# A Mamba layer with a mixture of experts on one core: another order of all operations, with all sixteen rounds written out

## The chip, the cores and the metric

The kernel runs on one core of a Trainium2 chip. The core has five engines that run side by side, each with an instruction queue of its own: TensorE (matmuls, PE in the profile, with its weight loads as PEld), VectorE (DVE), ScalarE (ACT), GpSimd (POOL) and SyncE (SP), which here only issues transfers. They meet through semaphores: an instruction raises a counter, and another one waits until the counter has reached a value. The metric is the device time of one execution in microseconds (us), as the median of several runs; lower is better.

## The reference, cut to what matters

The input is 32 sequences of 256 tokens with 128 channels. Two sublayers follow each other, each with a layer norm ahead and a residual around it.

```python
xr = x @ W_in;  xi, res = split(xr, 2)              # 128 -> 2 x 256
u = silu(causal_conv(xi, 4 taps) + conv_b)
dbc = u @ W_x                                       # 8 of delta, 16 of B, 16 of C
delta = softplus(dbc[:8] @ W_dt + b_dt)
for n in range(16):                                 # states
    h_n[t] = exp(delta * A_n)[t] * h_n[t-1] + (delta * u * B_n)[t]
    y += h_n * C_n
x = x + ((y + u * D) * silu(res)) @ W_out

scores = norm(x) @ gate_w.T;  top 2 of 8, softmax over the two
x = x + sum over e in 0..7 of cw[:, e] * (silu(norm(x) @ w1[e].T) @ w2[e].T)
```

All eight experts are computed for every token and weighted with `cw`, which is zero for six of them.

## The kernel before, in words

The work is cut into 16 rounds, r0 to r15, of two sequences (512 tokens) each. One round goes through all of the computation, but the rounds are laid over each other as in a pipeline: in a steady stretch TensorE works on the convolution of round i, the rows and states of rounds i-1 and i-2, and the experts of rounds i-4 and i-3.

For each of the 16 states n of a round: TensorE spreads row n of B over the partitions (`row_b`, L1737, into one of two banks of `rows`), VectorE multiplies it by `du` (`inputs`, L1248) and runs the scan (`scan`, L1258), with the factors `dA` that ScalarE has made by two exps (`decay`, L872). GpSimd multiplies the state by its row of C (`outputs`, L551), and TensorE adds it up while turning it (`sum_states`, L1758, eight turns). `row_b(j, n)` waits for scan n-2. `skip_in` (L1747) begins the sum of a round with u * D, which `skip` on ScalarE makes.

For each of the 8 experts: two hidden units (`hidden`, L1806 on TensorE, two matmuls each, and L906 on ScalarE, silu into `hid`), then `expert` (L1829, 16 matmuls), then `weight_expert` on VectorE (L1340) and `add_expert` on GpSimd (L591). hidden(j, e, f) is unit f of expert e of round j.

Around them: `turn_x`, `convolve` (L1682), `project_gate` (L1692), `project_bcd` (L1701), `take_high`, `take_middle`, `delta_rank` (L1727), `turn_y`, `project_out` (L1779), `turn_x2` and `score` on TensorE; norms, copies, `gate_silu`, `soft_parts` on ScalarE; `gating`, `residual`, `top_two` and statistics on VectorE; `add_soft`, `times_u`, `routing` and the deviations on GpSimd.

Six PSUM banks are shared. Where TensorE writes a bank, it first waits for the last reader of what was in it; the `use_...` entries in its order name these readers, so `hidden(three, 1, 0, use_hid(three, 0, 0))` waits until silu has read hidden(., 0, 0).

ScalarE's functions lie in two tables: exp and ln in one, silu in the other. A load of a table (ACT_TABLE_LOAD) stands ahead of the first activation that needs another one. It is put there when the kernel is built, and for silu it carries the line of the activation behind it (L906). The waits of a hidden unit on ScalarE are these two:

```python
wait(act, expert_done, j.count(E, e - 1))
act.wait_ge(hid_projected, j.count(E * FH, FH * e + f + 1))
nc.scalar.activation(hid[:, e % 2, f, :], bank(place(HIDDEN, j, e, f)), ACT.Silu).then_inc(hid_ready, 1)
```

The order of each engine is written out by hand (or by a planner, of which the kernel shows only the outcome): the first rounds, then a body `round_(i)` that `run` repeats, then the end. `run` writes the first bodies out and puts pairs of the others into a loop of the engine; inside it a round's semaphore values come from registers, outside they are constants. On TensorE and ScalarE rounds 6 to 15 of the body are five passes of that loop.

Of the kernel before, what the change touches and what calls it, by code (L numbers as in the profile page):

```python
# [43 lines left out]
HIDDEN = ("hidden", ((0, 1), (0, 1), (1, 0), (0, 0), (1, 0), (0, 1), (0, 0), (1, 0)))  # L44
# [5 lines left out]
MOVED = {("expert", 1, 0): 5, ("expert", 1, 1): 3, ("expert", 1, 2): 2, ("expert", 1, 4): 3, ("expert", 1, 5): 2,  # L50
         ("expert", 1, 6): 3, ("expert", 1, 7): 4, ("expert", 2, 0): 1, ("expert", 2, 1): 0, ("expert", 2, 2): 3,
         ("expert", 2, 3): 5, ("expert", 2, 4): 3, ("expert", 2, 5): 2, ("expert", 2, 6): 4, ("expert", 3, 1): 0,
         ("expert", 3, 2): 0, ("expert", 3, 4): 0, ("expert", 3, 5): 0, ("expert", 3, 7): 0,
         ("hidden", 1, 0, 1): 3, ("hidden", 1, 1, 0): 4, ("hidden", 1, 1, 1): 0, ("hidden", 1, 2, 0): 2,
         ("hidden", 1, 2, 1): 1, ("hidden", 1, 3, 0): 4, ("hidden", 1, 4, 1): 4, ("hidden", 1, 5, 0): 5,
         ("hidden", 1, 6, 0): 4, ("hidden", 1, 7, 0): 5, ("hidden", 1, 7, 1): 1, ("hidden", 2, 0, 0): 1,
         ("hidden", 2, 1, 1): 2, ("hidden", 2, 2, 0): 3, ("hidden", 2, 2, 1): 4, ("hidden", 2, 3, 0): 5,
         ("hidden", 2, 3, 1): 2, ("hidden", 2, 4, 0): 4, ("hidden", 2, 4, 1): 2, ("hidden", 2, 5, 0): 1,
         ("hidden", 2, 5, 1): 4, ("hidden", 2, 6, 0): 5, ("hidden", 2, 7, 0): 3, ("hidden", 2, 7, 1): 5,
         ("hidden", 3, 2, 1): 1, ("hidden", 3, 3, 0): 1, ("hidden", 3, 3, 1): 1, ("hidden", 3, 4, 1): 1,  # L60
         ("hidden", 3, 5, 0): 1, ("project_out", 1): 0, ("project_out", 2): 0, ("score", 1): 2}
# [30 lines left out]
def mamba_moe(nc, x, W_in, conv_w, conv_b, W_x, W_dt, b_dt, A_log, D, W_out, gate_wT, w1T, w2T, out):  # L92
# [15 lines left out]
    def run(eng, body, first, stages, stop):  # L108

        loop_first = max(first, stages + 2)  # L110
        pairs = (min(rounds, stop) - loop_first) // 2
        for i in range(first, loop_first):
            body(Round(i))
        with eng.Fori(0, pairs) as it:
            body(Round(loop_first, it))
            body(Round(loop_first + 1, it))
        for i in range(loop_first + 2 * pairs, stop):
            body(Round(i))
# [2265 lines left out]
```

## Time and profile before

| | |
|---|---|
| median of 3 runs | 1091.44 us (1090.85 to 1091.58) |
| profiled execution | 1092.1 us, span 1090.0 us |
| mean granted clock of TensorE | 0.978 |
| busy, share of the span | TensorE 95%, weight loads 70%, VectorE 93%, GpSimd 88%, ScalarE 83% |
| transfers | 84.12 MB, 77 GB/s on average |

The span is the time from the first to the last instruction; the profiled execution's own time is 2.1 us more. A matmul's end in the profile is modelled, and matmuls overlap by some 0.16 us, so the start of one and the start of the next tell what it costs. A wait is shown in brackets with what released it.

### The profile page before, as it was taken

The numbers are of one execution on the slowest core, as the hardware profiler recorded it, in microseconds if no ns is written. First come the engines' busy times: TensorE is split into PE (matmuls) and PEld (weight loads), VectorE is DVE, ScalarE is ACT, GpSimd is POOL, SyncE is SP. The second block draws the span as 40 slices with busy tenths as digits, with TensorE's granted clock in tenths as the row PEclk, the third lists the DMA queues.
The fourth block names the chain that finished last, engine by engine and source line by source line (L and its number), as shares of the span: only waits on it lengthen the run. The fifth ranks groups of instructions, "written<-read, shape, count | busy, mean of one in ns | idle before, by whom it ended". The sixth has DMA issues, their size and how long they took to land.

```text
span 1090.0 us, 18707 instructions
## 1 busy us (share of the span) xinstructions
PE 1040.8 (95%) x6150; PEld 758.0 (70%) x6150; DVE 1017.5 (93%) x1057; ACT 907.1 (83%) x1379; POOL 959.6 (88%) x890
## 2 busy tenths in 40 slices
PE   7787789999999999999999999999999999989998
PEld 4445466677777777777776777777777776767776
DVE  5999999999999999999999999999999999999822
ACT  4987867988989999998989899899989989875533
POOL 4688886999999999999999999999999999799934
PEclk9698989999999999999999999999999999989999
DMA  5332111122040312204031311403130130320000
GB/s 202 137 127 77 71 48 79 59 108 78 1 158 28 127 59 103 82 9 173 3 126 58 126 58 40 145 0 126 58 136 39 66 109 0 137 87 11 11 8 14
DMA packets 37364, 84.12 MB, mean 77 GB/s; under 512 B 3320, under 2 KB 28208, under 8 KB 28976
## 3 DMA queue, kind: packets, MB, share of 16 engines
q1 hardware_dynamic: 36880, 83.06, 21.4%
q8 instruction: 25, 0.41, 0.2%
q14 instruction: 43, 0.35, 0.1%
q10 hardware_dynamic: 416, 0.30, 0.1%
HBM read 78.63 MB, written 4.72 MB: 76 GB/s over the span
## 4 chain that ended last, share of the span: by engine, by line
PE 83%; DVE 9%; issue 4%; ACT 3%; DMA 0%; POOL 0%; DVEq 0%; ACTq 0%; POOLq 0%
PE work L1829 19%; PE work L1806 18%; PE y_ps L1758 18%; PE work L1682 8%; DVE h L1258 6%; PE rows L1737 4%; PE work L1779 3%; PE work L1666 2%; PE work L1701 2%; PE rows L1829 2%; PE work L1692 2%; PE rows L1806 1%; DVE rows L1248 1%; PE y_ps L1747 1%; PE work L1727 1%
## 5 line engine op out<-in xcount | busy, mean ns | idle before, releaser
L551 POOL TENSOR_TENSOR h<-h,c_rows 128x1024 f32<-128x1024 f32 x256 | 599.9, 2364 | 53.5 <-DVE h L1258 53.2
L1258 DVE TENSOR_TENSOR_SCAN h<-dA,rows 128x1024 f32<-128x1024 f32 x256 | 579.0, 2276 | 1.1
L872 ACT ACTIVATE dA<-delta,a_neg 128x510 f32<-128x510 f32 x512 | 325.7, 707 | 7.9 <-DVE h L1258 4.4
L1248 DVE TENSOR_TENSOR rows<-du,rows 128x1024 f32<-128x1024 f32 x256 | 306.7, 1214 | 4.9 <-PE rows L1737 4.9
L1758 PEld LDWEIGHTS y_ps<-ident,h 128*128 128x128 f32 x2048 | 241.2, 144 | 62.3 <-issue 34.5
L1758 PE MATMUL y_ps<-ident,h 128*128 128x128 f32 x2048 | 270.0, 278 | 10.3 <-POOL h L551 10.3
L1829 PEld LDWEIGHTS work<-w,hid 128*128 128x128 f32 x1856 | 223.3, 193 | 34.5 <-ACT hid L906 18.9
L1806 PE MATMUL work<-x2T,w 128*128 128x512 f32 x474 | 240.2, 602 | 2.9 <-ACT u L790 2.3
L1829 PE MATMUL work<-w,hid 128*128 128x128 f32 x1856 | 229.1, 277 | 2.4 <-ACT hid L906 2.2
L906 ACT ACTIVATE hid<-work 128x512 f32<-128x512 f32 x237 | 139.3, 596 | 65.5 <-PE work L1806 63.7
L591 POOL TENSOR_TENSOR x<-x,weighted 128x512 f32<-128x512 f32 x127 | 161.9, 1274 | 19.6 <-DVE weighted L1340 19.2
L1806 PEld LDWEIGHTS work<-x2T,w 128*128 128x128 f32 x474 | 82.2, 191 | 56.8 <-issue 19.0
L1737 PE MATMUL rows<-parts,select 96*128 96x512 bf16 x256 | 100.2, 392 | 21.9 <-DVE h L1258 20.4
L1682 PE MATMUL work<-xnT,w_conv 128*128 128x512 f32 x256 | 116.1, 596 | 0.5 <-ACT xnT L782 0.3
L756 ACT ACT_TABLE_LOAD x74 | 94.9, 1283 | 1.3
L906 ACT ACT_TABLE_LOAD x56 | 71.8, 1283 | 22.5 <-PE work L1806 16.7
L1340 DVE TENSOR_TENSOR weighted<-work,cw 128x512 f32<-128x512 f32 x116 | 78.4, 676 | 9.1 <-PE work L1829 7.2
L1682 PEld LDWEIGHTS work<-xnT,w_conv 128*128 128x128 f32 x256 | 47.3, 190 | 49.0 <-issue 47.8
L1737 PEld LDWEIGHTS rows<-parts,select 96*128 96x128 bf16 x256 | 25.4, 99 | 56.3 <-DVE h L1258 28.4
L542 POOL TENSOR_TENSOR du<-delta,u 128x1024 f32<-128x1024 f32 x15 | 35.4, 2360 | 1.8 <-POOL delta L535 1.3
L535 POOL TENSOR_TENSOR delta<-du,soft 128x1024 f32<-128x1024 f32 x15 | 35.4, 2362 | 0.0
L790 ACT ACTIVATE u<-work,conv_bias 128x512 f32<-128x512 f32 x32 | 22.0, 687 | 15.5 <-PE work L1682 15.3
(147 smaller groups left out, 941.7 us busy)
## 6 DMA issues: line engine op xcount, KB each, us to landing
c_rows<-c_dram SPq DMA_DIRECT2D x64, 1024.0 KB, 5.0
x_in<-in_x SPq DMA_DIRECT2D x16, 256.0 KB, 3.0
x_again<-in_x SPq DMA_DIRECT2D x16, 256.0 KB, 3.4
out<-x SPq DMA_DIRECT2D x15, 256.0 KB, 2.6
w<-in_w1T SPq DMA_DIRECT2D x1, 1024.0 KB, 4.8
w<-in_w2T SPq DMA_DIRECT2D x1, 1024.0 KB, 7.0
h<-in_conv_w SPq DMA_DIRECT2D x1, 512.0 KB, 4.9
c_dram<-bcd SPq DMA_DIRECT2D x16, 32.0 KB, 1.6
```

The lines of the kernel that those rows point to most:

```text
L551: nc.gpsimd.tensor_tensor(at, at, c_rows[:, n, :].unsqueeze(1).broadcast_to([P, H, T]), ALU.mult).then_inc(c_used, 1)
L591: nc.gpsimd.tensor_tensor(x1[:, j.odd], x1[:, j.odd], weighted[:, e % 2], ALU.add).then_inc(expert_added, 1)
L756: nc.scalar.preload_act_table_set("natural_log_exp_and_others")
L872: last = nc.scalar.activation(two_seqs(dA[:, n % RING, half, :])[:, :, 1:], two_seqs(delta[:, half, :])[:, :, 1:], ACT.Exp, scale=a_neg[:, ...
L906: nc.scalar.activation(hid[:, e % 2, f, :], bank(place(HIDDEN, j, e, f)), ACT.Silu).then_inc(hid_ready, 1)
L1248: nc.vector.tensor_tensor(rows[:, n % 2], du[:, j.odd], rows[:, n % 2, H - 1, :].unsqueeze(1).broadcast_to([P, H, T]), ALU.mult).then_inc( ...
L1258: nc.vector.tensor_tensor_scan(h[:, n % RING].rearrange("p h t -> p (h t)"), dA[:, n % RING].rearrange("p h t -> p (h t)"), rows[:, n % 2] ...
L1682: last = nc.tensor.matmul(two_seqs(work[:, CONV[half], :]), w_conv[:, k, half * P:(half + 1) * P], xnT[:, :, k:k + SEQ], start=(k == 0), s ...
L1737: nc.tensor.matmul(rows[:, n % 2, H - 1, :], select[:, n, :], parts[:, j.odd, :], start=True, stop=True).then_inc(b_ready, 1)
L1758: last = nc.tensor.matmul(y_ps[:, half, b, :], h[:, n % RING, half, b * P:(b + 1) * P], ident[:, :], is_transpose=True, start=False, stop= ...
L1806: nc.tensor.matmul(bank(place(HIDDEN, j, e, f)), w1[:, e, f, :], x2T[:, j.odd, :], start=True, stop=True).then_inc(hid_projected, 1)
L1829: last = nc.tensor.matmul(token_bank(place(EXPERT, j, e))[:, b, :], hid[:, e % 2, f, b * P:(b + 1) * P], w2[:, f, e, :], start=(f == 0), s ...
```

## The change

The loop of `run` goes: every body is written out, with its semaphore values as constants. And the order on every engine is another one: in the first rounds, in the body and at the end. The cut between first rounds and body also lies elsewhere (TensorE's body now begins at `sum_states(two, 6)`), which by itself moves nothing. The bank tables HIDDEN and MOVED follow the order. No operation is added or taken away. The core of the diff, by engine:

```diff
-    def run(eng, body, first, stages, stop):
-        loop_first = max(first, stages + 2)
-        pairs = (min(rounds, stop) - loop_first) // 2
-        for i in range(first, loop_first):
-            body(Round(i))
-        with eng.Fori(0, pairs) as it:
-            body(Round(loop_first, it))
-            body(Round(loop_first + 1, it))
-        for i in range(loop_first + 2 * pairs, stop):
+    def run(body, first, stop):
+        for i in range(first, stop):
             body(Round(i))
```

TensorE, body (waits on the left of a name left out; the steps that only changed their list of readers too):

```diff
                 expert(four, 3, use_hid(four, 4, 1))
+                expert(four, 4, use_dt(one, 1), use_hid(four, 4, 0))
+                hidden(four, 5, 0, use_expert(four, 3))
+                row_b(two, 12)
                 sum_states(two, 8)
-                expert(four, 4, use_dt(one, 1), use_hid(four, 4, 0))
-                row_b(two, 12)
-                hidden(four, 5, 0, use_expert(four, 3))
                 sum_states(two, 9)
                 hidden(four, 5, 1, use_expert(four, 4))
                 row_b(two, 13)
...
+                hidden(four, 7, 0, use_hid(four, 6, 1))
+                hidden(four, 7, 1, use_x2T(three), use_expert(four, 5))
...
                 sum_states(two, 11)
-                hidden(four, 7, 0, use_x2T(three), use_expert(four, 5))
-                hidden(four, 7, 1, use_xnT(i), use_hid(four, 6, 1))
+                score(three, use_hid(four, 7, 1), use_x2T(three))
                 row_b(two, 15)
-                score(three, use_hid(four, 7, 0), use_x2T(three))
                 sum_states(two, 12)
+                expert(four, 6, use_xnT(i), use_hid(four, 7, 0))
                 row_b(one, 0)
-                expert(four, 6, use_hid(four, 7, 1))
...
-                sum_states(two, 13)
-                row_b(one, 1)
-                convolve(i, 1, use_expert(four, 6), use_hid(four, 7, 1), use_xnT(i))
-                row_b(one, 2)
-                expert(four, 7, use_u(i, 0), use_scores(three), use_hid(four, 7, 0))
+                row_b(one, 1)
+                convolve(i, 1, use_expert(four, 6), use_xnT(i))
+                expert(four, 7, use_u(i, 0), use_scores(three), use_hid(four, 7, 1))
+                row_b(one, 2)
+                sum_states(two, 13)
                 sum_states(two, 14)
+                row_b(one, 3)
...
-                row_b(one, 3)
                 hidden(three, 0, 1, use_expert(four, 7), use_u(i, 0), use_scores(three))
                 sum_states(two, 15)
-                row_b(one, 4)
                 hidden(three, 1, 0, use_hid(three, 0, 0))
                 hidden(three, 1, 1, use_hid(three, 0, 1))
                 skip_in(one)
+                row_b(one, 4)
...
                 sum_states(one, 0)
                 sum_states(one, 1)
-                sum_states(one, 2)
                 row_b(one, 5)
                 expert(three, 0, use_gated(two), use_hid(three, 1, 0))
                 hidden(three, 2, 0, use_gated(two), use_hid(three, 1, 1))
                 row_b(one, 6)
                 hidden(three, 2, 1, use_expert(three, 0))
+                sum_states(one, 2)
                 expert(three, 1, use_hid(three, 2, 0))
-                row_b(one, 7)
...
+                row_b(one, 7)
                 expert(three, 2, use_expert(three, 1))
+                take_high(i)
+                row_b(one, 8)
                 sum_states(one, 3)
-                take_high(i)
                 sum_states(one, 4)
-                row_b(one, 8)
                 take_middle(i)
+                project_out(two, ...)
+                hidden(three, 3, 0, use_low(i), use_hid(three, 2, 1))
+                row_b(one, 9)
+                sum_states(one, 5)
+                project_gate(i, 0, ...)
+                delta_rank(i, 0, use_hid(three, 3, 0), use_low(i))
```

In the order of before, the last six of these are project_out, row_b(9), hidden(3, 0), sum_states(5), project_gate(0) and delta_rank(0). VectorE's body now begins with inputs 0 and 1, then scans 0 and 1, and goes on more often by twos; gating stands ahead of scan 4 as before, residual ahead of scan 8, top_two behind scan 14. GpSimd's body takes add_soft ahead of outputs(12) instead of behind it, times_u behind add_expert(4), routing ahead of outputs(0) of the next round instead of behind its outputs(2). ScalarE's body takes post_norm ahead of hidden(6, 0), pre_norm behind it, copy_xnT behind hidden(7, 1) and skip between the two conv_silu. SyncE:

```diff
-                three, four, five, seven = (i.later(-k) for k in (3, 4, 5, 7))
-                load_again(five)
-                load_c(four, 2)
-                store_c(three)
-                store_out(seven)
-                load_c(four, 3)
-                load_c(three, 0)
-                load_c(three, 1)
+                one, two, five = (i.later(-k) for k in (1, 2, 5))
+                load_c(two, 0)
                 load_x(i)
+                load_c(two, 1)
+                load_c(two, 2)
+                load_again(two)
+                store_c(one)
+                store_out(five)
+                load_c(two, 3)
```

Of the first rounds (TensorE, then ScalarE) and of the end (VectorE, then TensorE), what the prediction speaks of:

```diff
             row_b(r[0], 3)
+            row_b(r[0], 4)
+            skip_in(r[0])
+            row_b(r[0], 5)
             sum_states(r[0], 0)
...
-            skip(r[0])
             decay(r[0], 0)
...
             decay(r[0], 10)
+            skip(r[0])
...
-            weight_expert(r[14], 0)
...
             inputs(r[15], 15)
+            weight_expert(r[14], 0)
             scan(r[15], 15)
...
             expert(r[12], 6, use_hid(r[12], 7, 0))
             row_b(r[15], 0)
+            row_b(r[15], 1)
+            expert(r[12], 7, use_scores(r[13]))
+            row_b(r[15], 2)
             sum_states(r[14], 13)
...
+            hidden(r[14], 2, 1, use_expert(r[14], 0))
             sum_states(r[15], 15)
-            hidden(r[14], 2, 1, use_scan(r[15], 15))
```

## Rows read from the trace of the kernel before

**Rows 1.** The page: the chain that ended last, shares of the span by engine.

```profile
PE 83%; DVE 9%; issue 4%; ACT 3%; DMA 0%; POOL 0%; DVEq 0%; ACTq 0%; POOLq 0%
```

**Rows 2.** Busy time by stretch (columns in its first row).

```profile
core 0: us, PE busy (x) PEld busy (x) DVE busy (x) ACT busy (x) POOL busy (x), PEclk, DMA share, GB/s
31.60:60.00 28.40, 21.68 (x82) 12.76 (x83) 28.37 (x21) 25.73 (x41) 23.52 (x28) 0.76 0.21 65
...
204.89:269.55 64.66, 63.16 (x383) 46.20 (x383) 62.89 (x65) 57.48 (x89) 59.98 (x55) 1.00 0.22 79
332.50:395.25 62.75, 62.75 (x384) 46.45 (x383) 62.29 (x65) 57.53 (x88) 59.75 (x55) 1.00 0.24 81
395.25:458.48 63.23, 63.16 (x384) 46.18 (x383) 62.66 (x65) 57.72 (x89) 60.12 (x55) 1.00 0.22 80
...
1030.00:1090.00 60.00, 56.88 (x347) 42.51 (x346) 15.00 (x39) 22.76 (x39) 26.84 (x35) 1.00 0.04 10
```

**Rows 3.** Timeline of TensorE, looped round: start, duration, what, idle before.

```profile
606.23 1.02 PE L1806 MATMUL work<-x2T,w 128*128 128x512 f32 x2
...
608.44 2.05 PE L1829 MATMUL work<-w,hid 128*128 128x128 f32 x16
```

**Rows 4.** Timeline of TensorE, written round, the same place.

```profile
226.81 1.02 PE L1806 MATMUL work<-x2T,w 128*128 128x512 f32 x2
...
229.95 2.02 PE L1829 MATMUL work<-w,hid 128*128 128x128 f32 x16 [1.04 <-ACT hid L906]
```

**Rows 5.** Timeline of ScalarE, looped round, the same place.

```profile
606.49 1.28 ACT L906 ACT_TABLE_LOAD   x1 [0.74 <-PE work L1829]
607.79 1.31 ACT L906 ACTIVATE hid<-work 128x512 f32<-128x512 f32 x2
```

**Rows 6.** Timeline of ScalarE, written round, the same place.

```profile
227.92 1.28 ACT L906 ACT_TABLE_LOAD   x1 [1.53 <-PE work L1806]
229.21 1.08 ACT L906 ACTIVATE hid<-work 128x512 f32<-128x512 f32 x2
```

**Rows 7.** Timeline of TensorE, written round: hidden(1; 3, 0) and delta_rank(4; 0).

```profile
239.94 1.02 PE L1806 MATMUL work<-x2T,w 128*128 128x512 f32 x2
...
243.08 0.59 PE L1727 MATMUL work<-parts,w_dt 96*128 96x512 bf16 x2 [0.38 <-ACT hid L906]
```

**Rows 8.** Timeline of TensorE, written round, from hidden(1; 0, 0) to hidden(1; 1, 0).

```profile
215.57 1.02 PE L1806 MATMUL work<-x2T,w 128*128 128x512 f32 x2
216.43 0.38 PE L1737 MATMUL rows<-parts,select 96*128 96x512 bf16 x1
216.65 1.02 PE L1806 MATMUL work<-x2T,w 128*128 128x512 f32 x2
217.51 1.03 PE L1758 MATMUL y_ps<-ident,h 128*128 128x128 f32 x8
218.38 0.38 PE L1737 MATMUL rows<-parts,select 96*128 96x512 bf16 x1
218.62 1.55 PE L1806 MATMUL work<-x2T,w 128*128 128x512 f32 x3
```

**Rows 9.** Timeline of TensorE, written round: hidden(1; 5, 0) and hidden(1; 6, 0).

```profile
254.23 1.02 PE L1806 MATMUL work<-x2T,w 128*128 128x512 f32 x2
...
257.28 1.12 PE L1806 MATMUL work<-x2T,w 128*128 128x512 f32 x2
```

**Rows 10.** VectorE's waits from 31.6 to 204.9: us, times, longest.

```profile
DVE rows L1248 <- PE rows L1737: 2.9, 4, 1.4
```

**Rows 11.** Timeline of TensorE, end of the middle.

```profile
965.92 1.09 PE L1758 MATMUL y_ps<-ident,h 128*128 128x128 f32 x8 [2.63 <-POOL h L551]
...
969.02 0.61 PE L1737 MATMUL rows<-parts,select 96*128 96x512 bf16 x1 [1.65 <-DVE h L1258]
```

**Rows 12.** Timeline of VectorE, end.

```profile
978.60 1.23 DVE L1248 TENSOR_TENSOR rows<-du,rows 128x1024 f32<-128x1024 f32 x1 [1.17 <-PE rows L1737]
...
1029.59 0.67 DVE L1340 TENSOR_TENSOR weighted<-work,cw 128x512 f32<-128x512 f32 x1
```

More of the change, by code:

```diff
@@ L445, in _ @@
             load_c(r[3], 0)
+            load_again(r[3])
             load_c(r[3], 1)
-            load_x(r[6])
-            run(sp, round_, 7, 7, 19)
-            load_again(r[14])
+            load_c(r[3], 2)
+            store_c(r[4])
+            store_out(r[0])
+            load_c(r[3], 3)
+            run(round_, 6, 17)
+            load_c(r[15], 0)
+            load_c(r[15], 1)
             load_c(r[15], 2)
@@ L935, in round_ @@
                 hidden(four, 5, 1)
+                post_norm(three)
+                hidden(four, 6, 0)
                 pre_norm(i)
-                hidden(four, 6, 0)
-                post_norm(three)
                 hidden(four, 6, 1)
                 copy_x2T(three)
-                copy_xnT(i)
-                skip(one)
                 hidden(four, 7, 0)
                 hidden(four, 7, 1)
+                copy_xnT(i)
                 decay(one, 0)
@@ L951, in round_ @@
                 conv_silu(i, 0)
+                skip(one)
                 conv_silu(i, 1)
@@ L960, in round_ @@
                 decay(one, 7)
+                decay(one, 8)
+                decay(one, 9)
+                hidden(three, 2, 0)
+                hidden(three, 2, 1)
+                decay(one, 10)
+                decay(one, 11)
+                high(i)
+                copy_bcd(i)
+                decay(one, 12)
+                middle(i)
+                decay(one, 13)
             def lead_in():
@@ L1345, in round_ @@
                 three, four, five, six = (i.later(-k) for k in (3, 4, 5, 6))
-                inputs(four, 14)
-                scan(four, 13)
-                scan(four, 14)
-                top_two(five)
-                inputs(four, 15)
                 inputs(three, 0)
-                scan(four, 15)
-                weight_expert(six, 6)
+                inputs(three, 1)
                 scan(three, 0)
-                inputs(three, 1)
                 scan(three, 1)
@@ L1390, in round_ @@
                 weight_expert(five, 5)
+                inputs(three, 14)
+                scan(three, 13)
+                scan(three, 14)
+                top_two(four)
+                inputs(three, 15)
+                scan(three, 15)
+                weight_expert(five, 6)
             def split_dt_weights():
@@ L2135, in _ @@
[L2135 to L2141 removed]
+            expert(r[0], 4, use_gate(r[3], 0))
+            hidden(r[0], 5, 0, use_expert(r[0], 3))
+            sum_states(r[2], 8)
+            hidden(r[0], 5, 1, use_expert(r[0], 4))
+            delta_rank(r[3], 0, use_hid(r[0], 5, 0))
```

759 lines of the change are left out of this document (382 added, 377 removed).

## Prediction

> **What bounds the kernel now.** I read four views in this order. The chain of work that ended last says that TensorE carries 83% of the span and VectorE 9% [rows 1]. An average over stages can mislead, so I then cut the span into stretches, one from each round's first convolution to the next one's [rows 2]. There the reader is to see three things. In the steady part TensorE is busy for 62.75 of 62.75 us and VectorE for 62.29: both are full, TensorE sets the pace and VectorE has under half a microsecond to spare. Rounds alternate between 62.75 and 63.23 us, and the longer one holds the jump back of TensorE's loop, so the jump costs 0.43 to 0.48 us for every two rounds. The round from 204.89 us, where ScalarE's instructions are written out and the order on all engines is that of the loop, takes 64.66 us. That is 1.9 us more for the same work, and it is the row on which this prediction turns: why is the written round slower?
>
> The timeline of TensorE answers where. In the looped round expert(., 1) starts 2.21 us after hidden(., 2, 0) started [rows 3]; in the written round 3.14 us [rows 4], with 1.04 us named as a wait for ScalarE's `hid`. The timeline of ScalarE answers why. In the loop the activation table is loaded at 606.49, while hidden(., 2, 0) (begun at 606.23) is still running; the load was released by the expert's matmuls, that is by `expert_done`, and silu starts at 607.79, 1.56 us behind its matmul [rows 3, 5]. In the written round the load starts at 227.92, released by the hidden matmul itself (L1806), and silu starts at 229.21, 2.40 us behind its matmul [rows 4, 6]. So with waits on constants the table load stands behind the wait for `hid_projected`; with waits on registers it stands ahead of it. The code of `hidden` is the same. The 1.28 us of the load come into the path from TensorE to ScalarE and back each time silu's table is loaded for a hidden unit that has just been computed.
>
> The other places in a written round: delta_rank(., 0) starts 3.14 us after hidden(., 3, 0) [rows 7]; hidden(., 1, 0) starts 3.05 us after hidden(., 0, 0) [rows 8]; hidden(., 6, 0) starts 3.05 us after hidden(., 5, 0) [rows 9]. These distances, 3.05 to 3.14, are the same loop each time: 2.40 to silu, 0.60 for silu, the rest for the signal. Each stop, however short, also makes the matmuls behind it start some 0.1 us later: hidden(., 2, 1) to expert in the loop has such a row (2.05 us for an expert's 16 matmuls where an undisturbed one takes 1.95).
>
> **The change part by part.** TensorE's own work is not changed. From [rows 8] a hidden unit takes 0.86 us from start to start, a row of B 0.22, the 8 turns of one state 0.87; a gate projection takes the same 0.86 as a hidden unit. A steady round without its stop of 0.37 (0.27 before the expert, 0.10 after it, from [rows 3] against 0.86 + 0.22 + 0.86 = 1.94) is 62.75 - 0.37 = 62.38 us.
>
> *All rounds written out, and the new order of the middle.* Now every round has the late table load. What each place costs follows from what the new order puts between the two ends:
> - hidden(0,0) to hidden(1,0): two rows of B are taken out of this stretch (row 3 goes ahead, row 4 behind skip_in). Left are 0.86 + 0.86 + 0.87 = 2.59 us against the 3.05 needed: 0.46, and 0.10 behind it, 0.56.
> - hidden(2,0) to expert(1): sum_states(2) comes in, 1.94 + 0.87 = 2.81 against 3.05 to 3.14: 0.24 to 0.33, and 0.10, about 0.38.
> - hidden(3,0) to delta_rank(0): row 9 comes in, 0.86 + 0.22 + 0.87 + 0.86 = 2.81 against 3.14: 0.33.
> - hidden(5,0) to hidden(6,0): sum_states(8) and row 12 come in, 3.9 against 3.05: nothing.
> - turn_x2 to hidden(7,1) are now 1.30 us apart (four turns, half of a state's, and a hidden unit), about what a copy between them needs: bounded by nothing and the 0.1 of a short stop; I take nothing.
>
> The sum is 1.27, with the last bound 1.3 us a round. A check of the method on the written round of before: 1.20 + 0.10 at the expert, 3.14 - 2.59 = 0.55 at delta_rank, 0.24 + 0.10 at hidden(6,0), 0.10 behind hidden(1,0) give 2.29, and 64.66 - 62.38 = 2.28. So a new steady round is 62.38 + 1.3 = 63.7 us on TensorE. VectorE (62.3) and GpSimd (59.8) stay below that [rows 2].
>
> Twelve rounds of the expert work (those of r1 to r12) follow this pattern: 12 x 1.3 = 15.6 us. They lose what they had before: ten looped ones 0.37 each, 3.7; two written ones (r1, and r12 at 920 us, whose rows repeat those of r1) 2.28 and 2.2, 4.5; and the four jumps back of the five iterations, 4 x 0.43 = 1.7. Together 9.9, so the middle becomes 15.6 - 9.9 = 5.7 us longer.
>
> *Moves inside VectorE, GpSimd and SyncE.* VectorE's order now makes two inputs and then two scans more often. Its sum is the same, and a row of B is made at least 0.2 us before each input asks for it when I lay the starts of the new TensorE order beside the old ones; where it is not, VectorE now has 63.7 - 62.3 = 1.4 us a round to absorb it. The largest single delay of a row is that of row 4 (2.6 us), and its input also moves behind two scans. If that cover were gone it would cost VectorE those tenths. GpSimd moves routing ahead of outputs(0) and add_soft ahead of outputs(12); it has 3 us a round free. On SyncE, load_c(., 3) stands behind store_c and store_out, but is issued near scan 7 and read at scan 12; load_x now stands behind load_c(., 0). With the DMA engines busy for 0.22 to 0.24 of a round [rows 2] I cost these at nothing.
>
> *The first rounds.* The operations up to the steady part are the same, in an order that starts r0's experts earlier. In this stretch VectorE is full, so what can be won is its idle time: up to 204.9 us it waits 2.9 us for rows of B [rows 10]. The new order puts row 13 of r1 ahead of the convolution of r3 and hidden(0,1) ahead of sum_states(10), which speaks for fewer of these waits. Against it: skip(r0) on ScalarE stands behind eleven decays instead of ahead of them, and row 5 of r0 behind skip_in, in a stretch where the clock granted is 0.76 (matmuls at the lower of its two levels) [rows 2], where a turn of a state takes twice as long. Not shown by the trace; bounds are -2.9 (all these waits gone) and +2 (two more of a microsecond, as the longest here, 1.4). I take -1.0, nearer to the second bound than to the first since the clock works against it.
>
> *The end.* At 965.92 TensorE waits 2.63 us for a state from GpSimd and at 969.02 1.65 us for a scan, its clock drops, and VectorE then waits 1.17 us at 978.60 for row 4 of r15 behind hidden units [rows 11, 12]. In the new order expert(12,7) goes ahead of sum_states(14,13), expert(13,0) ahead of row 4, and input 4 stands behind weight_expert(13,0), so I take VectorE's 1.17 as gone. It gains weight_expert(14,0) ahead of the last scan, 0.6 [rows 12]. Behind the last sum_states TensorE has one hidden unit less, 0.86. So -1.17 + 0.6 - 0.86 = -1.4. Bounds: -3 (TensorE also keeps its clock) and +1 (the waits stay and only the weighting is added).
>
> **Sum.** 5.7 - 1.0 - 1.4 = +3.3 us on the profiled execution, 1092.1 us (span 1090.0), so 1095.4. The median of the runs is 0.66 lower: 1091.44 + 3.3 = 1094.7 us.
>
> The trace puts a table load at 1.28 us and silu 0.01 us behind it [rows 5, 6]. The Trainium skill (ScalarE: Activation LUTs, What ACT_TABLE_LOAD costs) gives 1283 ns for the load and about 1380 ns more for a drain at each switch. By the page, three late loads a round would cost another 3 x 1.38 us in each of twelve rounds; the trace agrees on the load and has no such drain, so the sum goes by the rows.
>
> **The rivals.**
> - *The new order has no stops from the late load* (this ends faster). Mechanism: the load is placed ahead of the wait again, or ScalarE is ready earlier than I read. For it: in the loop silu is 1.56 us behind. Against it: every written hidden unit with a load shows 2.40. Then the middle is 12 x 0.15 - 9.9 = -8.1 and the time 1091.44 - 8.1 - 2.4 = 1081. It decides from the stop per round: at (9.9 + 2.4) / 12 = 1.0 us the change is worth nothing, below 0.85 it is faster.
> - *Unrolling pays*: the jumps go, which the alternation of 62.75 and 63.23 us speaks for [rows 2], and the stops are half of what I count, which no row speaks for: 12 x 0.65 - 9.9 - 2.4 = -4.5, 1087. The Trainium skill (Runtime: NRT & Kernel Launch, Instruction fetch mechanics) says that a taken branch breaks sequential prefetch and that kernels prefer full unrolling. The trace agrees that the jump costs something, 0.43 us each.
> - *The gains at the ends cover the stops*: first rounds -2.9, end -3, 5.7 in the middle: -0.2, 1091.2, no difference. For it: the waits are there. Against it: all of it would have to go.
> - *The first rounds get worse*: +2, and the end gives nothing: 5.7 + 2 = +7.7, 1099.
> - *The written stream is too long to be fetched in time*: against it, the written last 60 us have TensorE busy for 56.88 [rows 2], with only known waits. I give it 2 in 100.
>
> **Chances.** Forecast (a longer middle, partly paid back) 0.45; worse first rounds or more stops 0.13; gains at the ends cover it 0.24; half the stops 0.10; no stops 0.08. A measurement of this kernel tells about 0.2%, 2.2 us, from no change. Faster 0.18, within it 0.26, slower 0.56. The likeliest case alone spans 1093 to 1098 (1.1 to 1.45 us a round). The range reaches into the others: 1086 to 1100.
>
> **What would show it.** Right: tables before silu in all rounds starting about 1.1 us behind the hidden matmul, silu 2.40 behind; waits for `hid` in each round before hidden(1,0), expert(1) and delta_rank(0); all steady rounds alike, 63.5 to 63.9 us, no alternation; VectorE idle 1.4 us a round. Wrong: steady rounds under 63.4; a table load released by `expert_done`; or a first stretch that reaches the convolution of r4 more than 3 us away from 204.7.

## The result and the profile after

The changed kernel takes 1103.11 us (1101.34 to 1103.72) beside 1091.51 us (1090.85 to 1092.08) for the kernel before in the same session: ratio 1.0107 [1.0092, 1.0122]. The direction is as predicted, and the time lies 3.1 us above the range. The profiled execution has a span of 1101.9 us and its own time is 1103.68 us, so it is to be set against 1090.0 and 1092.1.

The chain that ended last, by engine (it answers [rows 1]). ScalarE's share has grown from 3% to 12%: TensorE's way now leads through it.

```profile
PE 77%; ACT 12%; issue 5%; DVE 4%; POOL 2%; ACTq 0%; DVEq 0%; POOLq 0%
```

Busy time by stretch, columns as in [rows 2], cut from one round's first convolution to the next one's. The rounds at 335.8 and 399.6 answer to those at 332.5 and 395.25. They are alike, 63.80 us each, and TensorE is busy for 63.18 of it. (Busy time runs to a matmul's end, so it also covers part of a short stop.)

```profile
31.60:60.00 28.40, 17.20 (x82) 12.20 (x83) 26.01 (x23) 23.09 (x39) 20.32 (x24) 0.68 0.22 68
...
207.60:271.70 64.10, 63.48 (x383) 45.84 (x382) 63.59 (x66) 57.92 (x89) 59.84 (x55) 1.00 0.22 79
335.80:399.60 63.80, 63.18 (x383) 45.97 (x382) 62.79 (x65) 57.56 (x88) 59.58 (x55) 1.00 0.22 79
399.60:463.40 63.80, 63.18 (x383) 45.98 (x382) 62.79 (x65) 57.56 (x88) 59.86 (x55) 1.00 0.22 80
```

TensorE's timeline at hidden(2, 0), sum_states(2) and the expert of a steady round (it answers [rows 3, 4]). From 485.06 to 488.20 are 3.14 us, though the work in between is only 2.81.

```profile
485.06 1.02 PE L1835 MATMUL work<-x2T,w 128*128 128x512 f32 x2
485.92 0.38 PE L1766 MATMUL rows<-parts,select 96*128 96x512 bf16 x1
486.14 1.02 PE L1835 MATMUL work<-x2T,w 128*128 128x512 f32 x2
487.00 1.04 PE L1787 MATMUL y_ps<-ident,h 128*128 128x128 f32 x8
488.20 0.46 PE L1858 MATMUL work<-w,hid 128*128 128x128 f32 x2 [0.16 <-ACT hid L935]
```

ScalarE at the same place (it answers [rows 5, 6]): the load begins 1.10 us and silu 2.40 us behind the start of the matmul, the two distances of the written round of before.

```profile
486.16 1.28 ACT L935 ACT_TABLE_LOAD   x1 [0.87 <-PE work L1835]
487.46 1.09 ACT L935 ACTIVATE hid<-work 128x512 f32<-128x512 f32 x2
```

TensorE between hidden(0, 0) and hidden(1, 0) (it answers [rows 8]): hidden(0, 0) and (0, 1), the turns of a state, and then the wait; 474.47 to 477.52 are 3.05 us where the work is 2.59.

```profile
474.47 1.88 PE L1835 MATMUL work<-x2T,w 128*128 128x512 f32 x4
476.19 1.04 PE L1787 MATMUL y_ps<-ident,h 128*128 128x128 f32 x8
477.52 1.55 PE L1835 MATMUL work<-x2T,w 128*128 128x512 f32 x3 [0.29 <-ACT hid L935]
```

**Where the 11.9 us arose.** The starts of some convolutions on TensorE's timelines, and the ends of the spans, of both kernels and of the experiments told below, in us:

```
                     conv r1  conv r4  conv r15    end   r4 to r15  r15 to end
before                  48.5    204.7     898.9  1090.0     694.2     191.1
changed                 54.9    207.6     910.0  1101.9     702.4     191.9
e1  before, written     47.9    204.7     916.2  1107.4     711.5     191.2
e2  changed, looped     54.0    206.5     917.7  1108.3     711.2     190.6
e3  changed, early      53.6    204.7     893.6  1083.3     688.9     189.7
e4  before, wr., early  48.4    204.3     893.6  1083.2     689.3     189.6
e5  as e2, loop at 6    54.2    206.3     922.8  1112.0     716.5     189.2
e6  first rounds        48.9    205.9     911.6  1103.2     705.7     191.6
e7  first, early        48.5    204.4     897.7  1087.5     693.3     189.8
e8  before, early       48.8    204.7     895.5  1084.1     690.8     188.6
e9  skip first          52.3    204.7     907.1  1099.0     702.4     191.9
e10 weight late         53.2    205.2     907.7  1100.0     702.5     192.3
e11 early, skip, weight 52.2    203.2     892.1  1082.3     688.9     190.2
e12 before, loop at 7   47.6    204.4     898.4  1089.4     694.0     191.0
e13 changed, PE written 53.9    206.4     899.0  1088.3     692.6     189.3
e14 before, ACT written 48.0    205.0     916.0  1107.3     711.0     191.3
```

The last two columns are differences of the rounded starts and can be off by 0.1.

Against the kernel before, the changed one loses 2.9 us up to the convolution of r4, 8.3 from there to the one of r15, and 0.7 from there to the end (from the unrounded starts). In the same cut the forecast was -1.0, +6.6 (eleven of the twelve rounds) and -2.3 (the twelfth with the end).

### The profile page after: what moved, and what is told of

It is laid out like the page before. It is cut to its first block, busy times and chain, and to the rows that moved or that the text cites. A ratio compares the mean times of both kernels' runs of the same rounds, so it can differ in the third digit from the quotient of the medians.

```text
span 1101.9 us, 17455 instructions
## 1 busy us (share of the span) xinstructions
PE 1043.0 (95%) x6150; PEld 752.3 (68%) x6150; DVE 1021.4 (93%) x1057; ACT 906.6 (82%) x1379; POOL 958.3 (87%) x890
## 4 chain that ended last, share of the span: by engine, by line
PE 77%; ACT 12%; issue 5%; DVE 4%; POOL 2%; ACTq 0%; DVEq 0%; POOLq 0%
PE work L1858 18%; PE work L1835 16%; PE y_ps L1787 15%; PE work L1711 8%; PE rows L1766 4%; ACT dA L901 4%; ACT L935 2%; ACT hid L935 2%; DVE h L1287 2%; PE work L1695 2%; PE work L1808 2%; PE work L1730 2%; PE rows L1858 2%; PE rows L1835 1%; PE work L1721 1%
## 5 line engine op out<-in xcount | busy, mean ns | idle before, releaser
L1787 PE MATMUL y_ps<-ident,h 128*128 128x128 f32 x2048 | 262.2, 276 | 6.3 <-POOL h L550 6.3
L1835 PE MATMUL work<-x2T,w 128*128 128x512 f32 x474 | 237.7, 601 | 5.8 <-ACT hid L935 3.8
L1721 PE MATMUL work<-xnT,w_in 128*128 128x512 f32 x64 | 34.7, 625 | 1.6 <-issue 0.8
```

Of the source, the lines that this page charges most:

```text
L1787: last = nc.tensor.matmul(y_ps[:, half, b, :], h[:, n % RING, half, b * P:(b + 1) * P], ident[:, :], is_transpose=True, start=False, stop= ...
L1835: nc.tensor.matmul(bank(place(HIDDEN, j, e, f)), w1[:, e, f, :], x2T[:, j.odd, :], start=True, stop=True).then_inc(hid_projected, 1)
```

## The experiments

**e1: the order of before, its loops written out.** The functions `run` are replaced by those of the changed kernel, nothing else.

```diff
-            run(act, round_, 5, 4, 16)
+            run(round_, 5, 16)
...
```

> The order of the kernel before, its loops written out with constants; nothing else is changed. Theory (the silu table is loaded behind the wait for the matmul as soon as waits are constants): the ten looped rounds go from 62.97 us on average to the 64.66 us of the written round of before, +16.9, so about 1108 us, and every silu with a load starts 2.40 us behind its matmul. Rival (the form is free and only the order decides): the four jumps go, about 1.7 us less, 1089.8 us.

Measured: 1109.67 us (1107.84 to 1110.67), ratio 1.0155 [1.0136, 1.0173], steady rounds 64.65. Writing out costs the order of before 17 us; the new order, at 1103.11, is the better of the two for written rounds.

**e2: the changed order with the loops of before.**

```diff
-            run(round_, 5, 16)
+            run(pe, round_, 5, 5, 16)
...
```

> The new order with the loops of the kernel before (rounds 7 to 14 or so in loops). Theory: the looped rounds lose the late table load, 63.80 us each becomes about 62.7 with the jump shared out, some 8 to 10 rounds, so 1092 to 1095 us; what is left over the kernel before (1 to 4 us) is the new first rounds. Rival (the order itself causes the 63.8): the looped rounds stay at 63.8 plus the jump, 1105 us.

Measured: 1110.21 us (1109.28 to 1110.79), 1.016 [1.0143, 1.0177]. Both expectations missed. From convolution to convolution the looped rounds without TensorE's jump take 62.7 to 62.8 us, as the theory has it; those with one take 67.8 to 69.5. TensorE's timeline around the first jump:

```profile
496.58 0.60 PE L1763 MATMUL work<-parts,w_dt 96*128 96x512 bf16 x2
501.22 1.96 PE L1794 MATMUL y_ps<-ident,h 128*128 128x128 f32 x8 [4.05 <-issue]
```

"issue" says that TensorE waited for nothing that the profile shows. The trace's record of the taken branch there lasts 4.90 us, the two later ones 4.37 and 5.02; in the kernel before the four last 0.24, 0.22, 0.21 and 0.21. The eight turns behind the gap take 1.96 instead of 1.04 us.

**e3: the changed kernel with silu's table asked for ahead of both waits**, in `hidden`, `conv_silu` and `gate_silu`.

```diff
+            def silu_tables():
+                if tables[0] != "silu":
+                    nc.scalar.preload_act_table_set("silu_and_others")
+                tables[0] = "silu"
...
-                tables[0] = "silu"
+                silu_tables()
```

> The changed kernel with the silu table loaded explicitly ahead of both waits of the activation that needs it. Theory: the stops of 0.56, 0.41 and 0.32 us go in all rounds, a steady round is 62.4 to 62.6 us instead of 63.80, twelve rounds, so 15 us less, about 1088 us; first rounds stay some 5 us late. Rival (the load costs ScalarE the same wherever it stands, or silu is held by something else): 1103 us, silu still 2.40 us behind its matmul.

Measured: 1085.29 us (1084.91 to 1086.21), 0.9935 [0.9919, 0.9952]: 17.8 us less than the changed kernel by this one request in three places, and faster than before. ScalarE's timeline at the place of the rows above; the load now lies under the matmul (which begins at 476.59), and silu starts 1.53 us behind it:

```profile
476.82 1.28 ACT L791 ACT_TABLE_LOAD   x1
478.12 1.27 ACT L941 ACTIVATE hid<-work 128x512 f32<-128x512 f32 x2
```

Its TensorE, without a stop ahead of the expert at 479.41:

```profile
476.59 1.02 PE L1841 MATMUL work<-x2T,w 128*128 128x512 f32 x2
...
478.54 1.03 PE L1793 MATMUL y_ps<-ident,h 128*128 128x128 f32 x8
479.41 0.39 PE L1864 MATMUL work<-w,hid 128*128 128x128 f32 x2
```

Busy time of e3 in a window of the length of a steady round (62.57 us from convolution to convolution). TensorE is busy throughout and VectorE for 62.45 of 62.60: what is left in the middle is the work itself.

```profile
330.30:392.90 62.60, 62.60 (x383) 45.96 (x383) 62.45 (x65) 57.78 (x88) 59.96 (x55) 1.00 0.22 81
```

**e4: e1 with the same early table**, the edit of e3 on the written order of before.

> The order of before, written out, with the silu table loaded explicitly ahead of both waits. Theory: no stops from the load and no jumps: steady rounds of 62.4 to 62.8 us, and the two written rounds of before (64.66) fall to the same, so 1091.5 - 10 x 0.4 - 2 x 2 = 1083 to 1085 us. Rival (loading earlier only moves the time): as e1, about 1108 us.

Measured: 1084.75 us (1083.10 to 1085.64), 0.9925 [0.9908, 0.9942]. 25 us less than e1 for the same edit. With the table early the two orders are equal: rounds of 62.64 and 62.57 us.

**e5: e2 with TensorE's loop at another place.** By the code of `run` it begins at round 6 here and at round 7 in e2, so one round less is written out ahead of it; the expectation names the rounds wrongly, and the body that repeats is two rounds, not three.

```diff
-            run(pe, round_, 5, 5, 16)
+            run(pe, round_, 5, 4, 16)
```

> Changed order with its middle looped as in the second experiment, but TensorE's loop begins at round 6 instead of round 5 (one round more written out ahead of it, the same body of three rounds). If the 4.4 to 5.0 us of TensorE's taken jumps there come from where the loop's code lies, the jump changes: below 1 us each, and the time falls to about 1092 to 1098. If they come from the length of this loop's body or from its being a loop at all, they stay at 4 to 5 us each, and the time stays at 1108 to 1111.

Measured, in a single run: 1114.12 us. The four taken branches last 4.54, 4.29, 4.88 and 4.60 us. Whether the loop begins at 6 or 7 doesn't decide it.

**e6: the changed kernel with the first rounds of before** on TensorE, ScalarE, VectorE and GpSimd. For TensorE, the head of it:

```diff
             lead_in()
-            project_gate(r[0], 0, use_u(r[0], 0))
             row_b(r[0], 0)
+            project_gate(r[0], 0, use_u(r[0], 0))
             row_b(r[0], 1)
+            skip_in(r[0])
...
```

> Changed kernel with the order of the first rounds (up to the steady part) of the kernel before on TensorE, ScalarE, VectorE and GpSimd. Theory, that the new first rounds cost 5.1 us up to the scans of r3: the scan (r3, 0) begins at 208 to 209 instead of 213.4, steady rounds stay 63.8, and the time is 1097 to 1099 against 1103.1. Rival, that VectorE or TensorE make it up later in any case (no gain at the end): 1102 to 1104.

Measured: 1105.01 us (1102.97 to 1105.33), 1.0118 [1.0101, 1.0135]: no gain. The convolution of r1 starts at 48.9, 6.0 us earlier than in the changed kernel; at r4 1.7 us are left of that; and the round of r4 then takes 67.4 us instead of 64.1. The scan (r3, 0) begins at 211.7 us, where the theory had 208 to 209. TensorE there stops for 1.9 us ahead of row 4 of r3 and for 1.2 us ahead of expert(1, 1), where the changed kernel stops for nothing and 0.33 us. So the new middle doesn't fit behind the old first rounds, and this run doesn't price the first rounds by themselves.

**e7: e6 with the early table.**

> The sixth experiment's order with the silu table loaded ahead of both waits, as in the third. Theory, that the two add up: 1085.3 less 2.6 us (what the scan (r3, 0) of the third experiment, 210.4, is behind 208.2 of the fourth, with steady rounds of 62.57 against 62.64, -0.8 us in twelve rounds): 1082 to 1084, even with or up to 2 us below the fourth experiment's 1084.75. Rival, the two overlap or the joint adds waits: 1085 to 1087.

Measured: 1087.38 us (1087.03 to 1089.33), 0.9965 [0.9951, 0.9979]: 2 us more than e3 and 0.4 above the rival's band; the theory that the two add up has failed. The round of r4 takes 67.4 us, as in e6.

**e8: the kernel before with nothing but the early table**, loops kept.

> Kernel before, its loops kept, with nothing but the early load of the silu table. Theory: the ten looped rounds had the load ahead of the wait already, so they lose at most their stop of 0.37; the two written ones lose 2.28 and 2.2; the four jumps of 0.43 stay: 1092 less 4.5 to 8.2, so 1084 to 1088. Rival, the loop gains nothing and only the written rounds do: 1087 to 1088.

Measured: 1085.25 us (1083.91 to 1086.21), 0.9939 [0.9922, 0.9955]. From the convolution of r4 to that of r15 it takes 690.8 us, the kernel before 694.2: 1.9 us of the difference lie in the written round from r4 to r5 and 1.5 in the ten looped ones, 0.15 each, less than their stop of 0.37. The other 2.6 us of the profiled difference lie behind the convolution of r15, where the instructions are written out again.

**e9: the changed kernel with skip(r0) ahead of the decays.**

```diff
             lead_in()
+            skip(r[0])
             decay(r[0], 0)
...
-            skip(r[0])
```

> Changed kernel with one step moved back: skip(r0) stands ahead of the eleven decays on ScalarE again, as in the kernel before. Theory A, that this is what makes the first rounds late and that the lateness is carried through: skip_in(r0) no longer waits 4.1 us, the convolution of r1 starts at 49 to 51 us instead of 54.9, the one of r4 at 205 to 206 instead of 207.6, and the time is 1100 to 1101.5. Theory B, that the start of r0 is absorbed before the steady part and the late tables of the first rounds are what the 2.9 us at the convolution of r4 are: the convolution of r1 comes earlier all the same, the one of r4 stays within 1 us of 207, and the time is 1102 to 1103.7.

Measured: 1100.76 us (1100.04 to 1101.98), 1.0089 [1.0075, 1.0103]. Beside e10, whose first rounds are those of the changed kernel and which ran on the same chip, the convolution of r1 comes 0.9 us earlier and that of r4 0.5. But e10's first scan also begins 0.7 us earlier than e9's (30.1 and 30.8 us); counted from it, the two convolutions come 1.6 and 1.2 us earlier, and set against the mean of the five executions with the changed kernel's first rounds and late tables both come 2.1 us earlier. The time is 1.7 us below e10's and fell into theory A's band, and skip_in(r0) no longer waits. Of the places, r4's convolution (204.7) lies just below the band of 205 to 206, and r1's (52.3) is later than 49 to 51. Theory A holds in the main: skip is worth 1 to 2 us.

**e10: the changed kernel with the weighting behind the last scan.**

```diff
-            weight_expert(r[14], 0)
             scan(r[15], 15)
+            weight_expert(r[14], 0)
```

> Changed kernel with weight_expert(14,0) behind the last scan again. Theory: VectorE sets the pace in the last scans, so the last scan ends 0.6 us earlier and the end follows: span 1101.3, time 0.4 to 0.8 us less than 1103.1. Rival: TensorE has the expert's work to do in any case, and the hidden units that fill the gap make it no matter: last scan 0.6 earlier, end within 0.2 us of 1101.9.

Measured: 1102.45 us (1101.79 to 1103.18), 1.0105 [1.0090, 1.0121]. Counted from the convolution of r15, the last scan starts at 129.0 us instead of 129.6 and the span ends at 192.3 instead of 191.8. The time, 0.7 us less than the changed kernel's, lies in the theory's band, but not by its mechanism: in the profiled execution what the scan wins isn't handed on, and the end comes 0.5 us later; what is shorter there lies ahead of the convolution of r4.

**e11: e3 with both moves**, skip first and the weighting behind the last scan.

> The third experiment (changed order, silu's table loaded ahead of both waits) with the two steps of the ninth and tenth moved back. Theory A of the ninth: 1 to 2 us less than the third experiment's 1085.3, and 0.6 for the weighting: 1082.8 to 1084.2. Theory B: only the weighting, 1084.5 to 1085.3. Either would be about the time of the order of before with the same early tables, 1084.75.

Measured: 1085.21 us (1084.11 to 1085.82), 0.9945 [0.9932, 0.9959]. That is in theory B's band and not distinguishable from e3, e4 and e8. The convolution of r4 starts at 203.2 us, the earliest of all, 1.5 us ahead of e3; but the profiled execution is the fastest of its five (1084.11 to 1085.82), and the medians of e3 and e11 are equal. The end takes 190.2 instead of e3's 189.7, as in e10 longer with the weighting behind the scan.

**e12: the kernel before with TensorE's loop at round 7.**

```diff
-            run(pe, round_, 5, 4, 16)
+            run(pe, round_, 5, 5, 16)
```

> Kernel before with TensorE's loop beginning at round 7 instead of 6 (four passes instead of five, rounds 6 and 15 written out on TensorE). If the 0.2 us that its taken jump costs goes with what lies around the jump's target and not with the kernel, the jump changes to several microseconds and the time rises by 3 x 4 to 5 us to some 1104 to 1107. If it stays at 0.2 us: 1091 to 1093.

Measured, in a single run: 1091.21 us. The three taken branches last 0.24, 0.21 and 0.21 us. TensorE's timeline at the first: the matmul behind the jump comes 0.44 us after the one ahead of it, which lasts 0.38.

```profile
489.75 0.38 PE L1717 MATMUL work<-parts,minus 96*96 96x512 bf16 x1
490.19 1.04 PE L1779 MATMUL work<-w_out,yT 128*128 128x128 f32 x7
```

**e13: the changed order, looped on every engine but TensorE.** The edit is that of e2, but for TensorE.

```diff
-            run(round_, 5, 16)
+            run_written(round_, 5, 16)
...
```

`run_written` is the changed kernel's `run` under another name.

> Changed order with the loops of the second experiment on every engine but TensorE, whose rounds stay written out. The 4.4 to 5.0 us of TensorE's jumps cannot come up, and ScalarE waits on registers in its loop, with the table ahead. Theory (the late table on ScalarE is what the middle costs, and the order alone costs about what the first rounds do): all looped rounds at 62.8 to 62.9 us like the second experiment's undisturbed ones, no jump, the end as in the changed kernel; 1110.2 less 3 jumps of 5 to 6.5 us: 1091 to 1095. Rival (writing TensorE out costs time itself): 1098 to 1103.

Measured: 1090.34 us (1089.46 to 1091.14), 0.9985 [0.9975, 0.9994]. Slightly less than the theory's band. Busy time in two windows of a round's length (its looped rounds take 62.7 to 62.9 us from convolution to convolution):

```profile
397.00:459.80 62.80, 62.80 (x384) 45.96 (x384) 62.36 (x65) 57.89 (x89) 60.02 (x55) 1.00 0.23 81
459.80:522.60 62.80, 62.80 (x383) 45.95 (x382) 62.47 (x65) 57.73 (x88) 60.07 (x55) 1.00 0.22 81
```

**e14: the kernel before with ScalarE alone written out.**

```diff
-            run(act, round_, 5, 4, 16)
+            run_written(round_, 5, 16)
```

> Kernel before with ScalarE's rounds alone written out, so only its waits are on constants; the loops of the other engines stay. Theory: the whole loss of the first experiment (1109.7) is ScalarE's, and TensorE's four jumps of 0.43 stay: rounds of 64.65 and 65.1 in turn, 1109 to 1112. Rival (constants or unrolling on the other engines carry part of it): 1095 to 1105.

Measured: 1108.87 us (1107.86 to 1110.15), 1.0155 [1.0138, 1.0172], the ratio of e1. The looped rounds take 64.5 and 64.7 us in turn, where the theory had 64.65 and 65.1, and the time is 0.1 us below its band. ScalarE's and then TensorE's timeline at hidden(2, 0), which begins at 485.84: the load is again released by the hidden matmul and silu starts 2.40 us behind it.

```profile
486.95 1.28 ACT L911 ACT_TABLE_LOAD   x1 [1.53 <-PE work L1811]
488.24 1.09 ACT L911 ACTIVATE hid<-work 128x512 f32<-128x512 f32 x2
```

```profile
485.84 1.02 PE L1811 MATMUL work<-x2T,w 128*128 128x512 f32 x2
...
488.89 0.38 PE L1834 MATMUL work<-w,hid 128*128 128x128 f32 x1 [0.82 <-ACT hid L911]
```

## Why the prediction was right and where it was wrong

**The mechanism of the middle: right, and shown.** That waits on constants put silu's table behind the wait for `hid_projected` was read from one written round of before. e14 changes that on ScalarE alone and loses all of e1's 17 us; e13 leaves loops on ScalarE and writes TensorE out, and loses nothing; e3 keeps everything written, puts the load ahead, and wins 17.8 us. Neither written rounds as such nor the new order is slow in the middle: e13 is 1.8 us faster than the kernel before (in the profiled executions 1.7 us are lost ahead of the convolution of r4, 1.5 won up to that of r15 and 1.9 behind it); e3 and e4 differ by 0.5 us, within their spread. In every run constants and written-out rounds go together, so which of the two moves the load was not separated.

**The size of the middle: nearly right.** A steady round takes 63.80 us, 63.7 were forecast. The three stops are 0.46 + 0.10 ahead of hidden(1, 0) (0.56 forecast), 0.33 + 0.08 ahead of the expert (0.38), 0.32 ahead of delta_rank (0.33), and nothing ahead of hidden(6, 0), as forecast. The place at hidden(7, 1), which I had bounded by 0 and 0.1 and taken at nothing, costs 0.14; it costs the same 0.14 in e3, so the late table isn't its cause. From the convolution of r4 to that of r15 the changed kernel needs 702.4 us, 16.2 above eleven stopless rounds of 62.38, where the forecast had 14.3; before has 8.0 above them, where I had 7.7. That is 8.3 us (unrounded) instead of 6.6. Of the 16.2, eleven times 1.42 are 15.6, and 0.6 is what the first two rounds (64.1 each) have beyond the others; the size of a round's stops, 1.42 for 1.3, is most of the miss. VectorE idles 1.0 us a round (62.79 of 63.80 busy), where I had 1.4.

**The first rounds: the step that failed.** The term was -1.0 with bounds of -2.9 and +2; the profiled execution has +2.9, just inside the 3 us that I had named as a sign of being wrong. I booked a gain that no row priced, and put the two costs that came, skip behind the decays and the late table, at less than that gain or at nothing. The weighing was wrong by itself, too: I called -1.0 nearer to +2 than to -2.9, but it lies 1.9 from the one that gains and 3.0 from the one that loses. The parts below are counted from the first scan, since that scan begins anywhere from 30.1 to 30.8 us in executions of the new order.
- skip(r0) behind eleven decays: about 2 us in the profiled executions. In the five executions with the changed kernel's first rounds and late tables (changed, e2, e5, e10, e13) the convolution of r4 starts 175.1 to 176.9 us behind the first scan, 176.0 in the mean, in e9 173.9. With early tables it is 174.4 in e3 and 172.5 in e11. This was named, as half of the case "first rounds get worse". TensorE's timeline shows its 4.12 us wait, at the low clock, and behind it sums and the gate projection late:

```profile
44.09 1.97 PE L1776 MATMUL y_ps<-ident,ud 128*128 128x128 f32 x8 [4.12 <-ACT ud L889]
45.86 0.63 PE L1766 MATMUL rows<-parts,select 96*128 96x512 bf16 x1
46.28 3.62 PE L1787 MATMUL y_ps<-ident,h 128*128 128x128 f32 x16
...
52.70 1.02 PE L1721 MATMUL work<-xnT,w_in 128*128 128x512 f32 x2
...
54.90 1.55 PE L1711 MATMUL work<-xnT,w_conv 128*128 128x512 f32 x3 [0.52 <-ACT xnT L811]
```

- The late table: 1.4 us (e9 and e11, alike but for the table and the weighting at the end). I counted its stops from the first of the twelve rounds on. In the order of before the same step is smaller: 173.1 to 174.1 us with late tables (before, e1, e12, e14), 173.1 with early ones (e4, e8). That it is larger in the new order because r0's experts come forward into the first rounds is argued and not shown: e6 and e7, with the first rounds of before, differ by 1.2 us.
- The execution: 0.9 us. The changed kernel's 176.9 is the largest of the five; in its stretch from 31.6 to 60 us the granted clock is 0.68, in the other four 0.70 to 0.73, in before 0.76 [rows 2].

These are 4.4 us. Against them stand 0.9 us by which the first scan begins earlier than in before, and 0.6 us by which e11, without the two costs, is shorter than before (172.5 and 173.1): that is all that shows of the forecast gain, and it is less than the scatter of equal code.

The waits for rows of B that were to go did not go. VectorE's waits up to the convolution of r4 (it answers [rows 10]) are 4.5 us instead of 2.9, and there is a new one for GpSimd:

```profile
DVE rows L1277 <- PE rows L1766: 4.5, 6, 1.7
DVE rows L1277 <- POOL du L541: 1.9, 1, 1.9
```

Counted from the first scan, r1's convolution starts at 23.0 to 24.2 us in the six executions with skip behind the decays, at 21.4 and 21.5 in e11 and e9, and at 16.9 to 17.2 in the order of before. So skip explains about two of some 7 us. What the rest is was not isolated (one more state is summed ahead of the gate projection of r0), and it matters little: by r4, e9 is within 0.8 us of the kernel before.

**The end: wrong in sign.** -2.3 was forecast for the twelfth round with the end (-0.9 and -1.4), +0.7 came (191.8 us instead of 191.1, and 191.8 again in e9). The step that failed is that I added up what VectorE wins. It did win: its wait of 1.17 us [rows 12] became waits of 0.16 and 0.39:

```profile
990.01 0.69 DVE L1369 TENSOR_TENSOR weighted<-work,cw 128x512 f32<-128x512 f32 x1 [0.16 <-PE work L1858]
991.09 1.23 DVE L1277 TENSOR_TENSOR rows<-du,rows 128x1024 f32<-128x1024 f32 x1 [0.39 <-PE rows L1766]
```

But TensorE's work in the end is fixed and nearly without gaps from 990 us on, so that only its stops count, and these did not shrink. The timeline of TensorE there (it answers [rows 11]):

```profile
975.48 0.39 PE L1766 MATMUL rows<-parts,select 96*128 96x512 bf16 x1 [1.78 <-DVE h L1287]
...
980.51 0.39 PE L1766 MATMUL rows<-parts,select 96*128 96x512 bf16 x1 [2.86 <-DVE h L1287]
...
987.92 0.60 PE L1858 MATMUL work<-w,hid 128*128 128x128 f32 x3 [0.78 <-ACT hid L935]
```

That is 5.4 us where before had 2.63 and 1.65. From 990 us to the last sum TensorE stops for another 1.4 us or so in short pieces, in before for some 0.5. The hidden unit that no longer stands behind the last sum (0.86) was moved ahead of it, where TensorE is as full. And the weighting ahead of the last scan, priced at +0.6, helps by some 0.5 (e10, e11). The late table takes part here as well: with it early the end of the new order takes 189.7 us (e3) instead of 191.8, and the written order of before 189.6 (e4) instead of 191.2 (e1). So at the end the new order by itself is worth nothing against the old one.

**The rivals.** "No stops" fell in the changed kernel and came true in e3. "Unrolling pays": the jumps are worth 1.7 us to the kernel before and no more. "The first rounds get worse" at 1099 was the nearest, with a chance of 0.13; its mechanism, skip behind the decays, was real and worth about the +2 that I had for it, but the excess of the middle and the late table came on top. The range ended at 1100 since it took that rival's +2 with no excess in the middle; the three terms together were off by 3.9 + 1.7 + 3.0 = 8.6 us, all in one direction. The late table and the full TensorE, which I used for the middle, were left out of the first rounds and of the end.

## What to carry to other kernels

Where an activation table alternates, put its load by an explicit request ahead of the waits of the instruction that needs it, and look for it in the trace again whenever the form of those waits changes; here it was worth 18 to 25 us in kernels that are written out, and 6 us in the kernel with loops, of which 1.5 in the ten looped rounds and 4.5 in what stands written out around them. A mechanism found in the steady part is to be applied to the first and last rounds as well before these get terms of their own. In a stretch where one engine is full, only its stops count: a wait that another engine loses there is worth nothing, and must not be added.

## What the runs showed of the hardware

- A taken jump of TensorE lasts 0.2 us in the order of before (fifteen branches in before, e8, e12 and e14, loop at round 6 or 7) and 4.3 to 5.0 us in the changed order (seven branches, loop at round 7 or 6), with bodies of nearly the same number of recorded instructions, 1637 and 1639 with the weight loads. A round of before with a short one is 0.43 us longer than one without. ScalarE's, VectorE's, GpSimd's and SyncE's took 0.04 to 0.07 us in both. What goes with the difference is the fetching of instructions. The queue q8 of the profile brings TensorE's: it moves 25 blocks of 16 KB in the kernel before, 49 in all kernels with TensorE written out, 58 in e2 and 61 in e5. In the kernel before it moves none from 413 to 936 us, so the passes of TensorE's loop run without a fetch; in e2 and e5 it moves nine in each full pass, two of them in the gap at each jump. In the row of a queue the blocks come first, then MB. The queue in the whole of before, then in e2 from 496 to 501 us, the first gap:

```profile
q8 instruction: 25, 0.41, 0.2%
```

```profile
q8 instruction: 2, 0.03, 2.9%
```

- The Trainium skill (Runtime: NRT & Kernel Launch, Instruction fetch mechanics) says that a taken branch breaks sequential prefetch; the trace agrees for the seven long jumps, and in the fifteen short ones there is nothing to fetch. Why the one body stays on the core and the other doesn't is open. So is the length of the gap: in e2 the two blocks have come by 499.6 us and the turns begin at 501.2. The data transfers may have a part in it. In the 5 us ahead of each long jump they fill the DMA engines (share 1.00 to 1.04), ahead of the jumps of before and e12 the share is 0.12 to 0.20, and no run separates this.
- Behind each of these seven long jumps the eight turns take 1.96 to 1.97 us instead of 1.04: TensorE has fallen to the lower of the granted clock's two levels (0.50 from 501.2 to 503.2 us in e2).
- Equal code reaches the convolution of r4 up to 2.4 us apart from one execution to the next (205.2 to 207.6; 1.8 us apart when counted from the first scan), so a single profile says little about tenths in the first rounds, while the stretch from r4 to r15 repeats to 0.1 us (702.4, 702.4, 702.5).
